# Rewriting the opening program of a fused two-layer transformer kernel: projections by token half, and the first head pair's queries made inside it

## The reference

```python
c_q = hidden_states @ w_q_down                                   # 192 wide
q_nope = (c_q @ w_q_up_nope).reshape(b, s, H, DN).transpose(0, 2, 1, 3)
q_rope = (c_q @ w_q_up_rope).reshape(b, s, H, DR).transpose(0, 2, 1, 3)
c_kv = hidden_states @ w_kv_down                                 # 64 wide
k_rope = (hidden_states @ w_k_rope)[:, None]                     # 64 wide
q_rope, k_rope = rotate(q_rope), rotate(k_rope)                  # x1*c1 - x2*s2, x1*s2 + x2*c2
q_lat = jnp.einsum('bhsd,hdr->bhsr', q_nope, wuk)
scores = einsum(q_lat, c_kv) + einsum(q_rope, k_rope)            # scaled, causal, softmax
x = _layernorm(x + out @ w_out)
```

## Time and profile before

| | |
|---|---|
| median of 3 executions | 1504.21 us (1502.7 to 1506.7) |
| the profiled execution's own time | 1504.59 us |
| its span, first to last instruction | 1502.8 us |
| PE busy | 1422.0 us (95%) |
| DVE, ACT, POOL busy | 940.4, 813.0, 524.8 us |
| first projection matmul starts | 8.72 us |
| first score matmul starts | 56.34 us |

### The profile page before, as it was taken

How to read it: one execution, slowest core, us unless ns; L and a number is a source line. 1 busy time by engine, 2 the same in 40 slices (tenths; PEclk the granted TensorE clock), 3 DMA queues, 4 the chain that set the end, 5 groups by cost and what they waited for, 6 DMA issues and landing times. The chain is left out here.

```text
span 1502.8 us, 23934 instructions
## 1 busy us (share of the span) xinstructions
PE 1422.0 (95%) x8048; PEld 1011.7 (67%) x8048; DVE 940.4 (63%) x1530; ACT 813.0 (54%) x1730; POOL 524.8 (35%) x487
## 2 busy tenths in 40 slices
PE   5699999999999999999978998999999999999996
PEld 4567776776777776677656874555555558888885
DVE  4456655655665555566677647766666437777967
ACT  3566666666666565676543422565655665333433
POOL 0144454434445333444031144514041024444542
PEclk9799999999999999999989998999999999999999
DMA  5233344233334333333410044524335032000000
GB/s 183 75 44 45 46 52 53 33 51 39 42 48 53 38 47 48 43 40 41 88 57 1 1 57 71 84 32 71 45 59 121 14 131 108 1 0 1 7 22 28
DMA packets 61665, 75.90 MB, mean 51 GB/s; under 512 B 20640, under 2 KB 42144, under 8 KB 60704
## 3 DMA queue, kind: packets, MB, share of 16 engines
q1 hardware_dynamic: 57248, 64.55, 24.6%
q0 software_dynamic: 4352, 10.49, 4.9%
HBM read 42.49 MB, written 2.10 MB: 30 GB/s over the span
## 5 line engine op out<-in xcount | busy, mean ns | idle before, releaser
L1666 ACT ACTIVATE l_probs<-l_banks 128x512 f32<-128x512 f32 (+3 forms) x366 | 165.8, 495 | 137.1 <-PE l_banks L1610 91.4
L1706 DVE TENSOR_REDUCE pm<-l_sm 128x2 f32<-128x1024 f32 (+1 forms) x192 | 178.5, 956 | 93.2 <-PE l_sm L1580 60.8
L666 ACT ACTIVATE probs<-sc,nmax 128x128 f32<-128x128 f32 (+7 forms) x256 | 190.1, 743 | 72.3 <-DVE nmax L750 68.8
L750 DVE TENSOR_REDUCE nmax<-sc 128x1 f32<-128x128 f32 (+7 forms) x256 | 193.6, 756 | 32.4 <-PE sc L493 26.9
L674 ACT COPY pt<-tb 128x512 f32<-128x512 f32 (+3 forms) x256 | 129.4, 505 | 151.3 <-PE tb L507 150.3
L507 PE MATMUL tb<-ident,probs 128*128 128x128 f32 x1152 | 172.6, 275 | 2.0 <-ACT pt L674 1.1
L78 PE MATMUL sc<-k_h,q_h 128*128 128x512 f32 (+4 forms) x384 | 144.4, 376 | 10.4 <-DVE q_l L774 8.4
L507 PEld LDWEIGHTS tb<-ident,probs 128*128 128x128 f32 x1152 | 132.0, 141 | 13.5 <-DVE pt L758 3.8
L1607 PE MATMUL l_banks<-qk_bufs 128*128 128x512 f32 (+3 forms) x366 | 135.8, 413 | 2.4 <-DMA qk_bufs<-mT 2.0
L529 PE MATMUL mb<-pt,ckv 128*64 128x512 f32 (+2 forms) x736 | 131.7, 493 | 3.2 <-DVE x_tok L740 2.9
L78 PE MATMUL sc<-k_h,q_l 128*128 128x512 f32 (+4 forms) x384 | 132.4, 345 | 0.0
(11 more groups left out here) (289 smaller groups left out, 3094.4 us busy)
## 6 DMA issues: line engine op xcount, KB each, us to landing
gated_late<-in_gated SPq DMA_DIRECT2D x11, 768.0 KB, 13.4
wout<-in_w_out SPq DMA_DIRECT2D x16, 512.0 KB, 4.4
late<-late SPq DMA_DIRECT2D x128, 64.0 KB, 2.0
rb<-rT SPq DMA_DIRECT2D x248, 32.0 KB, 4.5
qk_bufs<-late SPq DMA_DIRECT2D x96, 64.0 KB, 5.0
qk_bufs<-late POOLq DMA_DIRECT2D x96, 64.0 KB, 5.6
nope_t<-in_nope_by_dim SPq DMA_DIRECT2D x16, 192.0 KB, 3.9
late<-in_gated SPq DMA_DIRECT2D x3, 768.0 KB, 7.8
```

Source lines behind the costliest of these rows:

```text
L666: act.activation(prob_row(n, s), score_row(n)[0], ACT.Exp, bias=nmax[:, s:s + 1], accum_out=ssum[:, n:n + 1]).then_inc(exped, 1)
L750: dve.tensor_reduce(nmax[:, n % 4:n % 4 + 1], row, axes, ALU.max, negate=True).then_inc(negmax, 1)
L1666: act.activation(probs[(NC * g + c) % RING][:, h, 0:w], e_slot(g, n)[:, 0:w], ACT.Exp).then_inc(exped, 1)
L1706: dve.tensor_reduce(pm[g % 2][:, :, s, i, half], slot(("m", g, n))[:, :, 0:w], AX.X, ALU.max, negate=True).then_inc(freed, 1)
```

## The change

The opening program is rewritten, and `before()` is gone from `stage_mla` on all engines.

- The projection goes by token half: all `k` of half 0, then all `k` of half 1. The copies and splits of half 0 lie beside the matmuls of half 1.
- Between the halves PE makes the first pair's weight (`nope_t` by `wuk`) in a bank of its own, `pw`. Weights and queries of the first pair have buffers of their own (`fa_f`, `fa_h`, `fa_l`, `fb_f`, `fb_hl`).
- The host also supplies the first pair's rotary weights with their 32-column halves swapped (`rope_first`, 256 columns for 128). A third query tile, TURNED, is thus the swapped rotary query. The 8 transfers of 32 rows that swapped them are gone, and VectorE reads both tiles from PSUM and multiplies by `cos` and `sin` in one instruction each, with the scale in it.
- The queries of each half follow the projection on PE (15 matmuls a half, for 10 before). High parts are made per half on ScalarE. The low parts of half 0 are made on GpSimd, those of half 1 on VectorE.
- GpSimd makes the low keys. SP copies the keys across by halves inside the opening program. Rows 64 to 127 of `cqb_l` come by a transfer.
- PE runs 16 transposes of the identity before the projection and 24 after the last query. Nothing reads what they write.
- `load_q` for the second pair is now the first instruction of SP in `stage_mla`.

The core of the diff:

```diff
         k_sw = al.sb("k_sw", [P, S])
+        fa_f, fb_f = al.sb("fa_f", [P, 3 * P]), al.sb("fb_f", [QL - P, 3 * P])
+        fa_h, fa_l = al.sb("fa_h", [P, 3 * P], F32R), al.sb("fa_l", [P, 3 * P], F32R)
+        fb_hl = al.sb("fb_hl", [P, 3 * P], F32R)
+        q_f = [keep.late[:, 4 + e, :] for e in range(2)]
+        r_f, r_sw = keep.late[:, 2, :], keep.late[:, 3, :]
+        q_h, q_l = keep.first_h, keep.first_l
         pj = [al.ps(f"pj{i}", [P, BANK]) for i in range(6)]
         pc = al.ps("pc", [P, ST, KVL])
-
+        pw = al.ps("pw", [P, BANK])
...
-                keep.pairs.load_q(sp, 0)
+                sp.dma_start(pairs.nope[:], io["nope_by_dim"][:, 0:2, :]).then_inc(pairs.wq_in, 16)
+                for w, r0, r1 in ((fa_f, 0, P), (fb_f, P, QL)):
+                    sp.dma_start(w[:, P:3 * P], io["rope_first"][r0:r1, :]).then_inc(pairs.wq_in, 16)
+                sp.dma_start(pairs.wuk[:], pairs.by_dim("w_uk", 0, DN)).then_inc(pairs.wq_in, 16)
                 sp.dma_start(keep.cos, io["cos"]).then_inc(rope_in, 16)
                 sp.dma_start(keep.sin, io["sin"]).then_inc(rope_in, 16)
-                keep.pairs.load_o(sp, 0)
+                pairs.load_o(sp, 0)
                 sp.dma_start(keep.x[:], io["x"].rearrange("b (j p) d -> p (b j) d", p=P)).then_inc(keep.x_in, 16)
+                for n in range(2):
+                    half = slice(n * BANK, (n + 1) * BANK)
+                    sp.wait_ge(dve_ev, 6 * n + 6)
+                    sp.dma_start(keep.cqb_l[64:128, half].bitcast(F32), keep.cqb_l[0:64, half].bitcast(F32)).then_inc(keep.x_in, 16)
+                    sp.wait_ge(act_ev, 5 * n + 5)
+                    sp.wait_ge(k_lo, n + 1)
+                    for dst, src in ((keep.k2_h, keep.k_h), (keep.k2_l, keep.k_l)):
+                        for a, b in ((0, 64), (64, 0)):
+                            sp.dma_start(dst[a:a + 64, half].bitcast(F32), src[b:b + 64, half].bitcast(F32)).then_inc(keep.x_in, 16)
...
+                def lower_keys(n):
+
+                    half = slice(n * BANK, (n + 1) * BANK)
+                    pool.wait_ge(act_ev, 5 * n + 5)
+                    pool.tensor_tensor(keep.k_l[:, half], k_f[:, half], keep.k_h[:, half].bitcast(F32),
+                                       ALU.subtract).then_inc(k_lo, 1)
+
+                lower_keys(0)
+                pool.wait_ge(sig.wsplit, 2)
+                pool.tensor_tensor(fa_l[:], fa_f[:], fa_h[:].bitcast(F32), ALU.subtract).then_inc(sig.wsplit, 1)
+                pool.wait_ge(sig.wsplit, 3)
+                pool.tensor_tensor(fb_hl[64:128, :], fb_f[:], fb_hl[0:64, :].bitcast(F32), ALU.subtract).then_inc(sig.wsplit, 1)
+                pool.wait_ge(sig.wsplit, 4)
+                lower_keys(1)
+                for e in range(2):
+                    pool.wait_ge(act_ev, 10 + e + 1)
+                    pool.tensor_tensor(q_l[e][:, 0:BANK], q_f[e][:, 0:BANK], q_h[e][:, 0:BANK].bitcast(F32),
+                                       ALU.subtract)
...
+                def query(n, t, cols, ok):
+
+                    half = slice(n * BANK, (n + 1) * BANK)
+                    three(pe, pj[3 * n + t][:], [
+                        (fa_h[:, cols], keep.cqa_h[:, half]), (fa_h[:, cols], keep.cqa_l[:, half]),
+                        (fa_l[:, cols], keep.cqa_h[:, half]), (fb_hl[:, cols], keep.cqb_hh[:, half]),
+                        (fb_hl[0:64, cols], keep.cqb_l[0:64, half])]).then_inc(ok, 1)
+
+                def queries(n):
+
+                    pe.wait_ge(act_ev, 5 * n + 4)
+                    pe.wait_ge(dve_ev, 6 * n + 6)
+                    query(n, 0, ROPE, sig.qp)
+                    query(n, 1, TURNED, proj_ps)
+                    query(n, 2, NOPE, sig.qp)
+
...
+                pe.wait_ge(const_ok, 5)
+                for i in range(16):
+                    pe.transpose(pj[i % 2][:, 0:P], keep.ident[:], keep.ident[:])
+                project(0)
+                pe.wait_ge(pairs.wq_in, 16 * pairs.NWQ)
+                for e in range(2):
+                    pe.matmul(pw[:, e * 64:e * 64 + 64], pairs.nope[:, e, 0:P], pairs.wuk[:, e, :], start=True, stop=True)
+                    last = pe.matmul(pw[0:64, P + e * 64:P + e * 64 + 64], pairs.nope[:, e, P:QL], pairs.wuk[:, e, :],
+                                     start=True, stop=True)
+                last.then_inc(sig.wlat_ps, 1)
+                project(1)
+                pe.wait_ge(sig.wsplit, 4)
+                queries(0)
+                pe.wait_ge(act_ev, 6)
...
+                queries(1)
+                pe.wait_ge(sig.mb_read[0], 1)
+                for i in range(24):
+                    pe.transpose(pw[:, i % 4 * P:(i % 4 + 1) * P], keep.ident[:], keep.ident[:])
...
+                def nope_part(n):
+
+                    half = slice(n * BANK, (n + 1) * BANK)
+                    act.wait_ge(sig.qp, 2 * n + 2)
+                    act.mul(q_f[0][0:64, half], pj[3 * n + 2][0:64, :], SCALE0).then_inc(sig.mb_read[n], 1)
+                    act.mul(q_f[1][64:128, half], pj[3 * n + 2][64:128, :], SCALE0).then_inc(sig.mb_read[n], 1)
+
+                def high_query(n, ok):
+
+                    half = slice(n * BANK, (n + 1) * BANK)
+                    act.wait_ge(sig.mb_read[n], 3 - n)
+                    for e in range(2):
+                        act.wait_ge(sig.qadd, 2 * n + e + 1)
+                        act.copy(q_h[e][:, half], q_f[e][:, half]).then_inc(ok, 1)
...
+                act.wait_ge(sig.wlat_ps, 1)
+                act.wait_ge(pairs.wq_in, 16 * pairs.NWQ)
+                act.copy(fa_f[:, 0:P], pw[:, 0:P]).then_inc(sig.wlat_ev, 1)
+                act.copy(fb_f[:, 0:P], pw[0:64, P:2 * P]).then_inc(sig.mb_read[0], 1)
+                act.wait_ge(sig.wlat_ev, 1)
+                act.wait_ge(sig.mb_read[0], 1)
+                act.copy(fa_h[:], fa_f[:]).then_inc(sig.wsplit, 1)
+                act.copy(fb_hl[0:64, :], fb_f[:]).then_inc(sig.wsplit, 1)
+                split_half(1)
+                nope_part(0)
                 act.wait_ge(ckv_ps, 1)
-                act.copy(keep.ckv[:], pc[:]).then_inc(done, 1)
+                act.copy(keep.ckv[:], pc[:])
+                high_query(0, act_ev)
+                nope_part(1)
+                high_query(1, sig.qh_ok)
...
+                def turn_query(n):
+
+                    half = slice(n * BANK, (n + 1) * BANK)
+                    dve.wait_ge(sig.qp, 2 * n + 1)
+                    dve.scalar_tensor_tensor(out=r_f[:, half], in0=pj[3 * n][:], scalar=SCALE0, in1=keep.cos[:, half],
+                                             op0=ALU.mult, op1=ALU.mult).then_inc(sig.qrot, 1)
+                    dve.wait_ge(proj_ps, 6 + n + 1)
+                    dve.scalar_tensor_tensor(out=r_sw[:, half], in0=pj[3 * n + 1][:], scalar=SCALE0, in1=keep.sin[:, half],
+                                             op0=ALU.mult, op1=ALU.mult).then_inc(sig.qrot, 1)
+                    dve.wait_ge(sig.qrot, 2 * n + 2)
+                    dve.tensor_tensor(q_f[0][64:128, half], r_f[64:128, half], r_sw[64:128, half], ALU.add).then_inc(sig.qadd, 1)
+                    dve.tensor_tensor(q_f[1][0:64, half], r_f[0:64, half], r_sw[0:64, half], ALU.add).then_inc(sig.qadd, 1)
...
+                for e in range(2):
+                    dve.wait_ge(sig.qh_ok, e + 1)
+                    dve.tensor_tensor(q_l[e][:, BANK:S], q_f[e][:, BANK:S], q_h[e][:, BANK:S].bitcast(F32),
+                                      ALU.subtract).then_inc(sig.ql_ok, 1)
...
+                load_q(-1, 0, 0)
...
-                def first_rope(k):
-
-                    half = slice(k * BANK, (k + 1) * BANK)
-                    dve.wait_ge(rope_sw[k], 64)
-                    dve.tensor_tensor(r_sw[:, half], r_sw[:, half], keep.sin[:, half], ALU.mult).then_inc(qrot, 1)
-                    dve.tensor_tensor(r_f[:, half], r_f[:, half], keep.cos[:, half], ALU.mult).then_inc(qrot, 1)
-                    dve.wait_ge(qrot, 2 * k + 2)
-                    dve.tensor_tensor(q_f[0][64:128, half], r_f[64:128, half], r_sw[64:128, half], ALU.add).then_inc(qadd, 1)
-                    dve.tensor_tensor(q_f[1][0:64, half], r_f[0:64, half], r_sw[0:64, half], ALU.add).then_inc(qadd, 1)
...
+    first = arrays["rope_pairs"][:, 0:P]
+    turned = first.reshape(QL, 2, 2, DR // 2)[:, :, ::-1].reshape(QL, P)
+    arrays["rope_first"] = np.ascontiguousarray(np.concatenate([first, turned], axis=1))
```

142 lines of the change are left out of this document (64 added, 78 removed).

## The result

The change brought the median from 1504.22 us to 1493.39 us (four executions of each: 1492.92 to 1495.79 after, 1502.7 to 1506.7 before). The ratio is 0.9933, with a 95% interval of 0.9921 to 0.9945. The kernel is faster by 10.8 us. The forecast was 16.7 us, 1487.5, with a range from 1484 to 1491.5: the direction was right and the time outside the range.

The account below looks back on a forecast made before the run. The prediction took PE to bound the kernel, with idle stretches in the opening relay. Its 15.2 us to the second pair's product plus 1.5 of clock gave 16.7 us: 1487.5 us after a 0.4 median shift, range 1484 to 1491.5.

Parts of the forecast that it names:

- T: End of both projections with the four weight products between the halves, forecast at 29.2 us.
- Step 1: Projection: half 1's matmuls cover half 0's copies and splits, so PE does not wait; end at 29.2 us.
- Step 2: From the projection's end through DVE to the stage boundary: first score at 40.3, 16.0 us earlier.
- Step 3: Second pair's weight product: waits about 0.8 us for its late loads, starts at 44.0, 15.2 us earlier.
- Step 4: Clock after the boundary: if PE stays at 2.4 GHz, weight product and following query gain 1.5 us.
- the transposes do nothing: Rival: the clock falls near the boundary, saving only 15.2 us, 1489.4 on the profiled execution's scale; chance 0.26.
- both rows work: Rival: the first transposes also raise the clock for the projection, 2.4 us more, 19.1 us in all; chance 0.18.
- Slow loads: Rival: loads at the boundary land slowly, 4.7 us more at the second pair's product, leaving 12.0 us; chance 0.07.
- no gain: Rival: something at a fixed time in the first round holds the gain back, 1504.6 us; chance 0.02.
- a slower kernel: Rival: the second score's last transfer lands after 57.5; one at 65 would cost 7.6 us; chance 0.02.
- late key copies: Key copies issued by 36 us, landing in 4.6, wanted at the second score, 41.4: under 1 us to spare.

Follow-up runs that it names:

- again: The changed kernel timed and profiled a second time, unaltered: 1491.63 us, ratio 0.9924 to the kernel before.
- by_chunk: The changed kernel with the projection's old loop order, chunks outside and halves inside, weight products behind it: 1501.73 us, ratio 0.9985 to the kernel before.
- full_rows: The changed kernel with all 128 rows for the fifth query matmul, VectorE writing the `cqb_l` copy itself, no transfer: 1493.26 us.
- early_load: The changed kernel with the second pair's query weights loaded inside the opening program, after the first weight product: 1490.48 us.
- combo: The changed kernel with both early_load's and full_rows' edits: 1486.24 us, ratio 0.9887 to the kernel before.
- combo_fill: As combo, with 34 in place of 24 transposes ahead of the boundary: 1487.51 us, ratio 0.9898 to the kernel before.

## Why the prediction was wrong

Forecast and two profiles of the changed kernel, as gains over the profile of before (us):

| | forecast | after | again |
|---|---|---|---|
| first query against T = 29.2 | 0 | -0.2 | +1.0 |
| first query to first score, against 11.1 | 0 | -2.4 | -2.4 |
| score to product, against 3.7 | 0 | +0.2 | 0.0 |
| product to query, against 4.2 | 0 | -1.7 | -0.6 |
| lead at the second pair's query | 16.7 | 12.8 | 14.7 |
| exchange and rotation | 0 | -1.5 | +0.2 |
| lead at the last round | 16.7 | 11.2 | 15.0 |

**Step 1 held.** Half 1 covers the splits of half 0, PE has no gap, and T came at 29.41 and 28.24. by_chunk shows what the cover is worth, 6 to 7 us at the score. T moves by a microsecond with the point at which the clock rises (12.0 in `again`, 14.6 in the kernel after). The 1.0 us of `again` in the table is such a shift, not a gain of the change.

**Step 2 is the term that failed, by 2.4 us, in every profile.** "15 matmuls, 3.45 us" took each at 0.23. One in five has 64 rows, and it and its followers cost 0.41 us a product: 30 matmuls and the small transposes took 9.7 us (39.09 - 29.41), for 7.6. The diff showed the rows (`[0:64]`), and I priced them by the common kind. PE thus became the later of the two, and what follows it went late with it. Timelines of ScalarE and VectorE in the kernel after:

```profile
39.20 0.59 ACT L288 ACTIVATE late<-pj 64x512 f32<-64x512 f32 x1 [2.25 <-PE pj L78]
39.81 0.59 ACT L289 ACTIVATE late<-pj 64x512 f32<-64x512 f32 x1
40.44 1.14 ACT L297 CAST q_h<-late 128x512 fp32r<-128x512 f32 x2
```

```profile
41.09 1.29 DVE L365 TENSOR_TENSOR q_l<-late,q_h 128x512 fp32r<-128x512 f32 x2 [0.79 <-ACT q_h L297]
```

ScalarE waits for the last query tile, scales its two parts to 40.40, makes the high parts, and VectorE ends the low parts at 42.38, for a score at 42.86. From the start of the 24 transposes to the score it took 3.8 us (39.09 to 42.86), for 3.5 in the forecast, so 2.1 us of the 2.4 are the matmuls. VectorE's rotation of half 1 ended at 40.3 (forecast 38.0), since it waited for its tiles too, but ScalarE was still the later one. The durations that I had doubted were right: the factor-and-product instruction took 0.67 to 0.69 us, no second pass. The boundary cost 0.48 us, for 0.33. full_rows gives 1.55 of the 2.35 us back; of the rest, 0.33 is the wait for the long addition on VectorE.

**Step 3 held.** Product 3.5 to 3.7 us after the score, as the landing of `wuk` sets it. The wait was 1.3 to 1.5 us and not 0.8, since at full clock PE comes to the product 2.0 us after the score (early_load) and not 2.9; early_load removes it.

**Step 4 failed as a condition, not as a size.** The 24 transposes hold the clock to the boundary, and the few short scores behind it let it go, wait or no wait: at about 45.7 in the kernel after, in the product in early_load and combo, and in ten of the eleven profiles in which it was still up at the first score. Only combo_fill kept it, and its query came 1.54 us sooner behind the product than in the kernel before. I had made "the transposes hold it" and "PE stays at full clock" one condition. The rival by which the transposes do nothing has the saving of that step right for the kernel after (none) and not for `again` (0.9 us), and its mechanism is refuted.

**The first transposes.** The rival "both rows work" is half right. The transposes can raise the clock, and 16 did in at least five of nine profiles. But what the prediction held against it came true: PE then idles for 3.1 to 3.4 us, and the clock was down again in the first chunk. 40 transposes leave no idle time and gave 1.5 us at the first query, not 2.4.

**The remainder.** Forecast 16.7, less 2.4 and 1.5, is 12.8. The two medians of the kernel are 10.8 and 12.2 (1503.87 - 1491.63). What lies between is the size of the exchange, 0 to 1.7 us by profile, and what happens behind the rounds, where the two profiles of one kernel part by 2.4 us. The first is located and its cause open. The second arises between 770 and 836 us of before: there the lead goes from 11.2 to 9.2 us in the kernel after and from 15.0 to 15.3 in `again`. By PEclk, PE stood at 1.2 GHz for 10.4 us between 755 and 835 in the one, 6.8 in the other, and 13.8, 7.0, 13.6 and 10.2 in the four profiles of before. So this part is scatter of the clock that the kernel before has as well, and nothing was run to move it. Slow loads, no gain, and a slower kernel did not occur; the late key copies delayed nothing.
